# Projecting and rotating a sequence one step earlier, with a shuffle for the second projection, in an attention and expert kernel on one core

## What is computed

```python
xn = layernorm(x)
x  = x + attn(xn) + ffn(xn)

# attn: 16 heads of 8, q and k rotated in pairs of features
qkv = xn @ Wqkv.T
r1, r2 = t1*cos - t2*sin, t1*sin + t2*cos        # t1, t2: even and odd features
scores = q_rot @ k_rot.T / sqrt(8) - |i-j| / xi * e_gate,  causal
out = (softmax(scores) @ v) @ Wo.T

# ffn: 8 attention experts, then 8 MLP experts, each with router weights
n1 = layernorm(xn) * ln1_w + ln1_b
rw = gating(n1)                                   # normalised logits, top 2, masked softmax
q, k, v = sum_e rw[e] * (n1 @ proj[e])            # for each of q, k, v
a  = softmax(q @ k.T / sqrt(128), causal) @ v
hs = xn + sum_e rw[e] * (a @ o_proj[e])
n2 = layernorm(hs) * ln2_w + ln2_b
out = hs + sum_e gating(n2)[e] * (gelu(n2 @ w1[e]) @ w2[e])
```

## Time and profile before

| | |
|---|---|
| median of 3 runs | 1389.3 us (1386.13 to 1389.54) |
| the profiled execution | 1386.97 us |
| its span, first to last instruction | 1385.1 us |
| mean granted clock of PE | 0.966 of full speed |
| PE busy | 1229.1 us, 89% |
| DVE busy | 1004.5 us, 73% |
| ACT busy | 707.4 us, 51% |
| POOL busy | 211.0 us, 15% |
| chain that ended last, by engine | PE 68%, DVE 16%, issue 9%, SP's queue 4%, DMA 2% |

### The profile page before, as it was taken

One profiled execution on the slowest core, in us unless ns is written; L12 is line 12 of the kernel. 1 busy time (PEld: TensorE's weight loads), 2 busy tenths in 40 slices (PEclk: granted clock), 3 DMA queues, 4 the chain that ended last, 5 costly groups with the idle time before them and its releaser, 6 DMA issues.

```text
span 1385.1 us, 33706 instructions
## 1 busy us (share of the span) xinstructions
PE 1229.1 (89%) x10780; PEld 938.4 (68%) x10780; DVE 1004.5 (73%) x3691; ACT 707.4 (51%) x1281; POOL 211.0 (15%) x325
## 2 busy tenths in 40 slices
PE   1249999999999999999999999999999979999998
PEld 0127777777777677777777777777777766777776
DVE  5547777777777777777777777777777657777653
ACT  1115555555555555555555555555555665555532
POOL 1011111121111222221111111112111200000000
PEclk9659999999999999999999999999999999999999
DMA  5312232222222222222322222222222106544344
GB/s 131 87 63 79 79 90 81 82 82 77 78 78 82 81 80 78 77 77 81 96 97 77 77 79 88 81 82 81 80 80 78 53 26 230 194 154 154 154 169 153
DMA packets 107942, 133.19 MB, mean 96 GB/s; under 512 B 18116, under 2 KB 87252, under 8 KB 99692
## 3 DMA queue, kind: packets, MB, share of 16 engines
q1 hardware_dynamic: 105668, 131.66, 29.6%
q10 hardware_dynamic: 2216, 0.80, 0.2%
HBM read 109.12 MB, written 21.54 MB: 94 GB/s over the span
## 4 chain that ended last, share of the span: by engine, by line
PE 68%; DVE 16%; issue 9%; SPq 4%; DMA 2%; ACT 1%; DVEq 0%; ACTq 0%
PE ps L1448 9%; PE ps L1493 9%; PE ps L1694 8%; PE ps L1449 8%; PE ps L1680 8%; PE ps L1321 4%; PE ps L1458 3%; PE ps L1425 2%; DVE mx L1070 2%; PE ps L1408 2%; SPq L415 2%; PE ps L1371 1%; PE ps L1507 1%; PE ps L1381 1%; DVE xn L894 1%
## 5 line engine op out<-in xcount | busy, mean ns | idle before, releaser
L1070 DVE TENSOR_REDUCE mx<-ps 128x4 f32<-128x1024 f32 (+1 forms) x192 | 234.9, 1223 | 89.4 <-PE ps L1381 80.0
L663 ACT ACTIVATE pr<-ps 128x1024 f32<-128x1024 f32 x192 | 195.8, 1020 | 138.4 <-PE ps L1408 93.7
L558 POOL TENSOR_TENSOR n1s<-rep,n1T 128x256 f32<-128x256 f32 x256 | 176.8, 728 | 254.3 <-DVE mpart L1084 254.3
L669 ACT ACTIVATE ps<-trn 128x1024 f32<-128x1024 bf16 x191 | 197.2, 1032 | 5.1
L1694 PEld LDWEIGHTS ps<-w2s,ats 128*128 128x128 f32 x1024 | 131.7, 192 | 49.8 <-issue 46.8
L1448 PE MATMUL ps<-n1s,wqk 128*128 128x256 f32 x512 | 163.0, 400 | 0.0
L1449 PE MATMUL ps<-n1s,wqk 128*128 128x256 f32 x512 | 152.7, 380 | 0.0
L1458 PE MATMUL ps<-wv,n1s 128*128 128x128 f32 x1024 | 141.6, 281 | 0.0
L1493 PE MATMUL ps<-wop,ats 128*128 128x128 f32 x1024 | 140.0, 294 | 0.0
L842 ACT ACTIVATE n1s<-ps 128x512 f32<-128x512 f32 x128 | 76.5, 597 | 122.6 <-PE ps L1680 121.5
L1694 PE MATMUL ps<-w2s,ats 128*128 128x128 f32 x1024 | 135.7, 276 | 0.5 <-DVE ats L1253 0.5
(11 more groups left out here) (228 smaller groups left out, 2038.3 us busy)
## 6 DMA issues: line engine op xcount, KB each, us to landing
rep<-scr_rw SPq DMA_DIRECT2D x32, 1024.0 KB, 5.0
stk<-scr_rw SPq DMA_DIRECT2D x16, 1024.0 KB, 8.1
stk<-scr_parts SPq DMA_DIRECT2D x896, 16.0 KB
scr_parts<-parts SPq DMA_DIRECT2D x64, 192.0 KB, 2.3
rots<-scr_rw SPq DMA_DIRECT2D x8, 1024.0 KB, 4.8
wqk<-scr_rw SPq DMA_DIRECT2D x8, 1024.0 KB, 8.9
stk<-scr_parts SPq DMA_DIRECT2D x128, 48.0 KB
xt<-in_x SPq DMA_DIRECT2D x32, 128.0 KB, 2.5
```

Source lines behind the costliest of these rows:

```text
L558: pool.tensor_tensor(n1s[:, e], rep[:, par, e], n1T[:, par], ALU.mult).then_inc(n1s_done, 1)
L663: act.activation(pr[:, Q, :, i], ps[:, S2[0]:S2[0] + NF], ACT.Exp).then_inc(exp_done, 1)
L669: act.activation(ps[:, S2[0]:S2[0] + NF], seeds[:, kind:kind + 1].broadcast_to((P, NF, 512)), ACT.Copy).then_inc(seed_done, 1)
L1070: dve.tensor_reduce(mx[:, min(i, 1)].rearrange("p (f h) -> p f h", f=NF)[:, :, h:h + n], ps[:, S1[0]:S1[0] + NF].rearrange("p f (h t) -> p ...
```

## The change

It changes where parts of a sequence's work stand, and four ways of doing them.

- **The front.** In step n, `norm_T` and `proj` now work on sequence g = n+3 and stand in the step's tail: the transposes ahead of `pv(n, u, 1)`, the projection behind `att_T`. They write to banks S1[0] and S1[1] (LATER), which pass one uses otherwise. DVE rotates g after `add_x`. The logits, the gating and `proj_v` of n+2 stay in step n. The load of x moves to the end of SP's step, for n+4.
- **Rotation.** `proj` makes only q and k, two matmuls instead of four. DVE multiplies both by the cosine, and gets the exchanged features by `stream_shuffle` from PSUM, which exchanges partition r and r+16 within each 32.
- **Pass one beside pass two.** `unit1(n+1, 0)` is the first thing in a step, and each slot of pass two stands directly behind a unit. `row_max(n+2, 0)` is taken at the end of DVE's step, ahead of the casts of the rotation; the others at links 1, 6, 13 and 17 of the gating chain.
- **Banks.** `weights_T` and `max_T` use bank G1, and PE waits until ACT has read both before the output projection starts there.
- **ACT.** q and k, and the first values, are copied after the fourth exponential. One Copy takes both transposes.
- **Stacks.** Slots with the same part are filled by one DMA from a source with a repeated dimension: 14 DMAs per half and sequence where there were 20.
- **Prologue.** Loads have semaphores of their own and another order; big weights come later. POOL makes the bias rows and the ones of the key stacks, ACT casts masks, the norms of the router's matrices run between the links of the layer norm. Half of the first stack DMAs go out of ACT's queue.

The core of the diff:

```diff
-Q_SLOTS = ((0, 1, 0), (1, 1, 0), (2, 1, 0), (3, 1, 1), (4, 1, 1), (5, 1, 2))
-K_SLOTS = ((0, 3, 0), (3, 2, 0), (5, 1, 0))
+Q_SLOTS = ((0, 3, 1, 0), (3, 2, 1, 1), (5, 1, 1, 2))
+K_SLOTS = ((0, 1, 3, 0), (3, 1, 2, 0), (5, 1, 1, 0))
+SWAP = [r ^ H for r in range(2 * H)]
-GATE_MAX_AT = (7, 12, 17, 22)
+GATE_MAX_AT = (1, 6, 13, 17)
...
+        FIRST, LATER = (G0, PVB), (S1[0], S1[1])
...
+        def part_rows(b, par, Q, f):
+            hh = slice(HG * Q, HG * Q + HG)
+            for side, dst, slots in ((0, qst, Q_SLOTS), (1, kst, K_SLOTS)):
+                v = scr_parts[par, side].rearrange("p d h t -> (p d) h t")[:, HH * f + HG * Q:HH * f + HG * Q + HG]
+                for first, times, n, part in slots:
+                    r = KR * f + R_PARTS + DH * first
+                    src = v[DH * part:DH * (part + n)].rearrange("(o r) h t -> o r h t", o=1)
+                    yield dst[r:r + DH * n * times, par, hh], src.broadcast_to((times, DH * n, HG, S))
...
-            def rotate(b, beside=None):
-                c = Chain(dve, rot_chain, b, ROT_LINKS, beside)
-                dve.wait_ge(rot_q_out, b + 1)
-                c.link(dve.tensor_tensor(rott[:, 0], ps[:, G1].rearrange("p (a t) -> p a t", a=2), cs[:, 0], ALU.mult))
-                c.add(dve.tensor_tensor(rot[:, 0], rott[:, 0, 0], rott[:, 0, 1], ALU.add))
-                dve.wait_ge(rot_k_out, b + 1)
-                c.link(dve.tensor_tensor(rott[:, 1], ps[:, G1].rearrange("p (a t) -> p a t", a=2), cs[:, 1], ALU.mult))
-                c.link(dve.tensor_tensor(rot[:, 1], rott[:, 1, 0], rott[:, 1, 1], ALU.add))
+            def rotate(b, banks):
+                c = Chain(dve, rot_chain, b, ROT_LINKS)
+                both = ps[:, banks[1]].rearrange("p (a t) -> p a t", a=2)
+                dve.wait_ge(rot_out, b + 1)
+                c.add(dve.tensor_tensor(rott, both, cs[:, :, 0], ALU.mult))
+                c.add(dve.stream_shuffle(swapped, both, SWAP))
+                yield
+                c.wait()
+                c.link(dve.tensor_tensor(swapped, swapped, cs[:, :, 1], ALU.mult))
+                c.link(dve.tensor_tensor(rot, rott, swapped, ALU.add))
+                yield
...
                 def beside_gating(k):
...
-                    if k == 11:
+                    if k == 15:
+                        soft_max(n)
+                    if k == 18:
                         normalise(n, 0)
-                    if k == 14:
-                        soft_max(n)
-                    if k == 20:
+                    if k == 28:
                         soft_norm(n)
...
                 add_x(n, u)
+                turn = rotate(n + 3, LATER) if n_x == 3 else iter(())
+                next(turn, None)
+                next(turn, None)
+                if n_x >= 2:
+                    row_max(n + 2, 0)
+                run(turn)
                 add_hs(n, u)
...
-            def proj(b, side, prev):
+            def proj(b, banks, prev):
                 pe.wait_ge(xnT_done, b + 1)
                 prev()
-                for k in range(2):
-                    ins = mm(ps[:, G1, k * S:(k + 1) * S], wa[:, 2 * side + k], xnT[:], start=True, stop=True)
+                for side in range(2):
+                    ins = mm(ps[:, banks[1], side * S:(side + 1) * S], wa[:, 2 * side], xnT[:], start=True, stop=True)
...
+                if n_x == 3:
+                    norm_T(g, LATER, lambda: pe.wait_ge(s1_read, UNITS * f))
                 pv(n, u, 1)
...
                 att_T(n)
+                if n_x == 3:
+                    proj(g, LATER, lambda: None)
+                if n_x >= 2:
+                    pe.wait_ge(rwT_done, f + 1)
+                if n_x:
+                    pe.wait_ge(mT_done, n + 2)
                 oe(n, 0)
```

473 lines of the change are left out of this document (290 added, 183 removed).

## The result

| | before | after |
|---|---|---|
| median (lowest to highest, runs) | 1388.0 us (1386.1 to 1389.5, 4) | 1228.95 us (1228.75 to 1229.8, 4) |
| ratio, 95% interval | | 0.8856 (0.884 to 0.8871) |
| profiled execution, its span | 1386.97, 1385.1 | 1229.05, 1227.3 |
| start of step 0 (its first slot of pass two) | 95.8 (96.25) | 66.1 (66.89) |
| period of steps 1 to 28 | 32.73 | 28.39 |

Predicted were 1246 us and a range of 1230 to 1287. The span fell by 157.8 us where the sum said 143.2.

The account below looks back on a forecast made before the run. PE, busy 1229.1 of 1385.1 us, was taken as the bound. 1385.1 - 62.7 (waits) - 33.1 (PE work) - 14.4 (clock) - 31 (prologue) - 2 (end) = 1241.9 us span, forecast as 1246 us; range 1230 to 1287.

Parts of the forecast that it names:

- The waits: PE's four idle waits in each step nearly go, from 2.34 us to 0.25 left, over 30 steps: -62.7 us.
- The walk of the step: One step traced from its first matmul with handovers of 0.05 to 0.1 us; the gating chain closes at 21.5 us.
- Clock: Steps 1 to 28: with no long idle piece left, PE's clock no longer falls below 1.00: -14.4 us.
- PE's work per step: PE's busy time falls by 1.06 us a step, 29.87 to 28.81; -33.1 us including step 29's dropped transposes and projection.
- The two matmuls: Projection in each step: one of two disappears, the groups taking 0.86 and 1.06 us in the chain of waits.
- the change of type: Slots stand directly behind units in each step, so one of seven bf16-to-fp32 changes on PE goes: 0.20 us a step.
- DVE's slack: DVE would have 26.9 us of work a step against PE's 28.81, shuffle taken at 0.65 us.
- waits only change places: Rival, chance 0.13: PE-DVE handovers in the steps keep 1.2 us of waits a step and the clock gain fails: 1289 us.
- Prologue: Before step 0: reordered loads and stack DMAs from two queues bring its start from 95.8 to about 65: -31 us.
- End: Step 31: exponential goes ahead of expert norms on ScalarE, so DVE's 2.24 us wait before the softmax's reciprocal goes: -2 us.

Follow-up runs that it names:

- e11: Changed kernel without the third bf16 part of the rotated queries and keys (last subtraction covers one column instead of 256 per side): 1222.8 us.
- e14: Changed kernel with six single slot copies, router weights first in step 31, ScalarE's last stack copies later, rotation's first cast on POOL, eight memsets on DVE: 1220.6 us.
- e9: Changed kernel with slot 1 of pass two one pair of expert projections later, not directly behind unit 1 of pass one: 1263.5 us.
- e3: Changed kernel with one more row maximum of 128x512 on DVE near the start of each step, result unused: 1244.5 us.
- e7: Changed kernel with ScalarE's last six stack copies of the prologue issued behind the maxima and second weights instead of ahead: 1225.1 us.
- e5: Changed kernel with a stack's six query slots loaded by six copies instead of three with a repeated first dimension: 1227.5 us.
- e6: Changed kernel with the expert pass's first router weights' transpose and second logits ahead of experts 2 and 3 of step 31's output projection: 1227.7 us.

## Why the prediction was right in kind and short in size

- **The waits** (-62.7): right. 0.25 us a step was left, and 0.25 was measured. The walk of the step held to a few tenths: weights' transpose 22.4 us into the step (22.9 predicted), gating chain closed at 21.4 (21.5). What e11 and e14 add is that half of the 0.25 is DVE's lateness at unit 2, which goes with 0.43 to 0.46 less on DVE.
- **Clock** (-14.4): right, 1.00 in all 28 steps.
- **PE's work per step** is the step that failed: "29.87 - 1.06 = 28.81". Measured: 28.14. The two matmuls (0.86) are there, and so is the change of type (0.20; 0.24 in e9). What is missing is 0.67: the prediction charged a wait with its idle time alone and put the rest at nothing. PE's rows of the kernel before, and then DVE's, the last part of the maxima (start us, us):

```profile
642.57 0.71 PE L1458 MATMUL ps<-wv,n1s 128*128 128x128 f32 x4
643.95 0.55 PE L1476 MATMUL ps<-ident,sp 128*128 128x128 f32 x3 [0.67 <-ACT sp L690]
647.12 0.38 PE L1484 MATMUL ps<-spT,vs 128*128 128x128 f32 x2
647.34 0.38 PE L1437 MATMUL ps<-ident,ov 128*128 128x128 f32 x2
649.02 0.27 PE L1354 MATMUL ps<-ident,gt 128*16 128x128 f32 x1 [1.30 <-DVE gt L1051]
649.15 0.68 PE L1344 MATMUL ps<-wa,xnT 128*128 128x128 f32 x4
649.80 0.29 PE L1393 MATMUL ps<-identb,mpart 128*128 128x128 bf16 x2
```

```profile
649.55 0.19 DVE L1084 TENSOR_TENSOR mpart<-mres,mpart 128x32 bf16<-128x32 f32 x1
```

  The pair at 647.12 gives way after 0.22; the one at 647.34, alike, stands for its whole 0.38 in front of the wait. The value projection takes 649.80 - 649.15 = 0.65, where the changed kernel has 0.45: PE waited there for the maxima's parts, ready at 649.74, and the profile counts no idle for it, since the matmul in front had not ended. Busy time of PE by group in one step, averaged over the steps at full clock (14 before, 26 after):

| group | before | after | difference |
|---|---|---|---|
| projection | 1.83 | 0.97 | -0.86 |
| expert values | 4.13 | 3.77 | -0.36 |
| softmax's transposes | 0.55 | 0.33 | -0.22 |
| transposes ahead of the gating wait | 0.38 | 0.22 | -0.16 |
| value projection | 0.65 | 0.45 | -0.20 |
| units of pass one | 2.34 | 2.25 | -0.09 |
| heads' transposes | 0.33 | 0.40 | +0.08 |
| expert q and k | 7.60 | 7.67 | +0.07 |
| logits | 0.11 | 0.17 | +0.06 |
| all others | | | -0.02 |

  Three waits took 0.16 each with them, 0.49 (expert values, softmax's transposes, transposes ahead of gating); the other 0.20 of the expert values is the change of type. The fourth, for the heads, is in both kernels. The value projection's 0.20 is 0.13 of the wait that shows no idle and 0.07 of a slower start. The slower start of what stood behind a wait is 0.06 at the softmax's transposes and 0.09 at a unit. Against these stand 0.21 that the new order brings back (heads' transposes, q and k, logits). The balance is 0.63 of the 0.67. 28 x 0.67 = 18.7 us is the whole miss of the steps; with it the sum would have been 1246 - 18.7 = 1227.
- **DVE's slack**: "26.9 against 28.81". DVE was busy 26.1 (26.3 in the step shown), so the number was not too low, though it came about by two errors: it began from 26.4, where the earlier trace rows has 25.07 in such a step, and DVE's work rose by 1.00 a step (703.75 to 731.81 us in the 28 steps), not 0.50. What failed is what I took from it. 2 us of idle a step do not mean that 0.5 more is free (e3): slack is to be read at the instruction that PE waits for. The rival "waits only change places" was nearer than its 0.13 says: PE already waits 0.13 a step for a maximum, so DVE has no margin at that place.
- **Prologue** (-31): -29.7, by a walk with unit 0 at 34.6 (35.3), second parts at 48 (46.0), step 0 at 65 (66.1). ScalarE's issuing ahead of the maxima held step 0 back by 2.3 us (e7), and the fewer copies that I credited saved nothing (e5).
- **End** (-2): failed in sign, +0.2. The heads' transposes of step 31 came 1.8 us earlier, but the change also put the expert pass's weights behind two experts; e6 gets 1.3 back.
- **Not foreseen at all**: that any change to DVE's instruction count could cost 135 us. The change happened to land on the good side by three instructions, and none of my rivals had it.

## What to carry to other kernels

When a change takes waits away from TensorE, count for each wait its idle time, what the matmul in front of it adds to "busy" by standing alone (here 0.16 us between fp32 matmuls, 0.07 in front of a bf16 unit), the slower start behind it (up to 0.09), and the lower clock where one follows. Look also for waits that show no idle: a group that takes longer than the same group elsewhere. And count what the new order brings back. Read slack not from an engine's idle total but by asking at which instruction the other engine waits, and by adding half a microsecond there. And where a loop's body is longer than a block of instructions, compare the packets of the instruction queues and look for idle time released by "issue" at the jump back, before any difference is put down to the edit.

## What the runs showed of the hardware beyond that

- A shuffle of 128x512 fp32 out of PSUM within groups of 32 partitions: 0.73 us, with a mask load of 0.01 ahead of it; the fp32 multiply of 128x512 out of SBUF that reads its result took 0.88, against 0.69 for the one that reads PSUM.
- The time to issue did not follow the number of copies: 12, some with a repeated dimension, took 6.66 us, 18 for the same bytes 6.20.
- POOL multiplies 128x512 fp32 by ones into bf16 in 1.04 us beside a running row maximum of DVE, which stayed at 1.23.
